# Two graph layers for 16 batch elements: the second layer's attention product as three fp32r terms in place of full f32

## What is computed

```python
feat_proj = jnp.einsum('bnh,oh->bno', feats, fc_w) + fc_b
q = jnp.einsum('bnh,oh->bno', feat_proj, q_w) + q_b
k = jnp.einsum('bnh,oh->bno', feat_proj, k_w) + k_b
logits = q + jnp.swapaxes(k, 2, 1)
masked = logits + (1.0 - adj_mat) * NEG_INF
masked = jnp.where(masked >= 0, masked, LEAKY_SLOPE * masked)
atten = jax.nn.softmax(masked, axis=-1)
out = jnp.einsum('bnm,bmh->bnh', atten, feat_proj)
return out + feats
```

## Time and profile before

| | |
|---|---|
| median of 3 runs | 969.0 us (968.88 to 969.69) |
| profiled execution, its own time | 967.7 us |
| its span, first to last instruction | 965.4 us |
| mean granted clock of PE | 0.988 |
| instructions | 22082 |
| busy: PE / ACT / DVE / POOL | 929.8 / 796.7 / 768.6 / 300.4 us |

### The profile page before, as it was taken

One profiled execution on the slowest core, in us unless ns is written; L12 is line 12 of the kernel. 1 busy time (PEld: TensorE's weight loads), 2 busy tenths in 40 slices (PEclk: granted clock), 3 DMA queues, 4 the chain that ended last, 5 costly groups with the idle time before them and its releaser, 6 DMA issues. The chain is left out here.

```text
span 965.4 us, 22082 instructions
## 1 busy us (share of the span) xinstructions
PE 929.8 (96%) x7432; PEld 776.6 (80%) x7432; DVE 768.6 (80%) x2012; ACT 796.7 (83%) x1900; POOL 300.4 (31%) x408
## 2 busy tenths in 40 slices
PE   5889999999999999999999999999999999999966
PEld 4668788788878878888887888888788888887854
DVE  4687979788797988879788887978879797887832
ACT  3768989889897998989888897988889798887923
POOL 0012334323243431424342142433223343322441
PEclk9999999999999999999999999999999999999988
DMA  6677767476675747666574766657467765746100
GB/s 188 140 134 130 132 106 114 128 117 150 110 132 101 117 124 117 140 120 124 111 116 120 121 127 127 118 122 117 126 112 131 130 102 134 116 110 110 44 23 22
DMA packets 74718, 112.59 MB, mean 117 GB/s; under 512 B 7024, under 2 KB 33648, under 8 KB 74608
## 3 DMA queue, kind: packets, MB, share of 16 engines
q1 hardware_dynamic: 74608, 111.18, 59.7%
HBM read 52.44 MB, written 8.39 MB: 63 GB/s over the span
## 5 line engine op out<-in xcount | busy, mean ns | idle before, releaser
L975 DVE CUSTOM_DVE_ANT_0 sm_bank<-sm_bank,masks 128x512 f32<-128x512 f32 x512 | 352.4, 698 | 116.9 <-PE sm_bank L529 113.2
L731 ACT ACTIVATE e<-sm_bank,row_min 128x512 f32<-128x512 f32 x512 | 356.2, 698 | 33.0 <-DVE row_min L975 33.0
L539 PE MATMUL et_bank<-ident,e 128*128 128x128 f32 x2048 | 308.5, 273 | 3.2 <-DVE e_t L983 1.9
L539 PEld LDWEIGHTS et_bank<-ident,e 128*128 128x128 f32 x2048 | 252.1, 140 | 42.2 <-issue 6.8
L529 PE MATMUL sm_bank<-k_stack,q_stack 96*128 96x512 f32 x512 | 247.7, 484 | 5.6 <-DMA k_stack<-kt_lo 3.2
L723 ACT COPY e_t<-et_bank 128x512 f32<-128x512 f32 x272 | 161.2, 593 | 17.6 <-PE et_bank L539 15.9
L983 DVE COPY e_t<-et_bank 128x512 f32<-128x512 f32 x240 | 164.4, 685 | 11.4 <-PE et_bank L539 9.8
L529 PEld LDWEIGHTS sm_bank<-k_stack,q_stack 96*128 96x128 f32 x512 | 97.0, 190 | 36.2 <-issue 26.5
L475 PE MATMUL o_bank<-e_t,v 128*32 128x256 f32 x2048 | 123.8, 382 | 0.0
L508 PE MATMUL shared<-feat,z 128*128 128x256 f32 x512 | 121.8, 381 | 0.8 <-ACT z L669 0.8
L731 ACT ACTIVATION_READ_ACCUMULATOR e<-sm_bank,row_min 128x1 f32 x512 | 107.4, 210 | 0.0
(11 more groups left out here) (112 smaller groups left out, 1576.6 us busy)
## 6 DMA issues: line engine op xcount, KB each, us to landing
adj_in<-in_adj SPq DMA_DIRECT2D x32, 1024.0 KB, 5.5
q_stack<-qt_hi SPq DMA_DIRECT2D x62, 256.0 KB, 8.0
k_stack<-kt_hi SPq DMA_DIRECT2D x62, 256.0 KB, 7.8
x_in<-in_x SPq DMA_DIRECT2D x16, 512.0 KB, 6.4
h<-in_x SPq DMA_DIRECT2D x16, 512.0 KB, 3.8
out_y<-h SPq DMA_DIRECT2D x32, 256.0 KB, 6.7
q_stack<-qt_lo SPq DMA_DIRECT2D x31, 256.0 KB, 7.1
k_stack<-kt_lo SPq DMA_DIRECT2D x31, 256.0 KB, 11.1
```

The lines of the kernel that those rows point to most:

```text
L539: last = nc.tensor.transpose(et_bank[n % TURNED][:, c * P:(c + 1) * P], e[:, n % ROOM, c * P:(c + 1) * P], ident[:, :])
L731: nc.scalar.activation(e[:, k, :], sm_bank[n % SCORED][:, :], ACT.Exp, scale=-1.0, bias=row_min[:, k:k + 1], accum_out=row_sum[:, g, qt, i ...
L975: nc.vector.tensor_tensor_reduce(bank[:, :], bank[:, :], mask[b % 2][:, qt * N:(qt + 1) * N], 1.0, -LOWEST, ALU.add, ALU.min, row_min[:, k ...
```

## The change

The `at` steps become sums of three fp32r terms, as the projections are: 12 products of one pass for each block of 128 rows in place of 4 full f32 products. For that, `feat` becomes `feat_hi` and `feat_lo`, and the transposed z goes into new tiles `zt_hi` and `zt_lo` instead of back into z. ACT's copies write the hi parts; DVE gets two new kinds of step, `feat_lo0`, `feat_lo1` (two subtractions of 128x256 each) and `et_lo0` to `et_lo3` (one of 128x512 each). The readers that free a shared bank change with it. All five tables, DVE_COPIED (15 tiles before, 14 after), BANK, and the order of steps within a tile are laid out anew. The core of the diff:

```diff
-DVE_COPIED = (0, 3, 5, 6, 13, 14, 15, 18, 22, 24, 25, 26, 27, 28, 29)
+DVE_COPIED = (1, 3, 4, 6, 7, 13, 14, 15, 17, 21, 22, 24, 25, 31)
-FIRST_QK, AFTER_QK = 15, 17
+FIRST_QK, AFTER_QK = 14, 18
 PE_AT = {
-    "at3": 64, "et1": 65, "k1": 2, "rb1": 36, "pv3": 36, "at0": 69, "v1": 6, "at1": 73, "v0": 9, "xt1": -22, "op1": 44,
-    "xt0": -18, "op0": 46, "k0": -17, "q0": -16, "pv0": 17, "ht1": 50, "ht0": 50, "rb0": 21, "fc0": 53, "fc1": 54,
-    "kb": 56, "pv1": 24, "q1": -5, "pv2": 29, "et2": 62, "et3": 62, "at2": 63, "et0": 63}
+    "et1": 65, "v0": 5, "v1": 8, "xt1": -21, "pv1": 24, "q1": -5, "pv2": 29, "et3": 61, "et0": 63, "at3": 64,
+    "rb1": 35, "at1": 74, "op1": 45, "op0": 45, "ht1": 51, "fc0": 53, "fc1": 54, "kb": 55, "rb0": 25, "et2": 60,
+    "k1": 1, "pv3": 36, "at0": 73, "xt0": -21, "q0": -18, "k0": -16, "pv0": 18, "ht0": 50, "at2": 62}
 ACT_AT = {
+    "k_hi1": 2, "v1": 8, "x_hi1": -22, "q_hi0": -17, "h_hi0": 50, "logit0": 56, "lexp2": 58, "et3": 60, "et0": 62,
+    "et1": 64, "rs1": 34, "v0": 7, "hn0": 49, "hn1": 49, "h_hi1": 50, "feat0": 52, "feat1": 53, "logit1": 56,
+    "rs0": 24, "q_hi1": -6, "et2": 59, "o_hi0": 34, "o_hi1": 35, "x_hi0": -22, "k_hi0": -16, "logit2": 55,
+    "logit3": 55, "l_negmax": 56, "lexp3": 58, "lexp0": 59, "lexp1": 61}
 DVE_AT = {
-    "l_recip": 64, "rc1": 33, "fin1": 66, "k_lo1": 4, "o_n1": 38, "fin0": 73, "x_lo1": -20, "h_add1": 45, "stats1": 45,
-    "x_lo0": -18, "h_add0": 46, "stats0": 46, "moments": 46, "k_lo0": -17, "q_lo0": -16, "rc0": 18, "h_lo1": 50,
-    "h_lo0": 50, "q_dot0": 54, "q_dot1": 56, "l_max0": 56, "l_max1": 56, "o_n0": 26, "q_lo1": -4, "mask1": -1,
-    "mask0": -1}
+    "fin1": 64, "rc1": 33, "et_lo1": 66, "k_lo1": 4, "o_n1": 37, "x_lo1": -21, "x_lo0": -20, "q_lo0": -15,
+    "q_dot0": 54, "feat_lo0": 54, "l_max0": 56, "q_lo1": -4, "et_lo2": 61, "fin0": 74, "h_add1": 45, "stats0": 46,
+    "q_dot1": 54, "mask0": -2, "stats1": 45, "h_add0": 45, "moments": 46, "k_lo0": -15, "rc0": 18, "h_lo0": 51,
+    "h_lo1": 51, "l_max1": 55, "feat_lo1": 57, "o_n0": 26, "et_lo3": 61, "mask1": -2, "l_recip": 63, "et_lo0": 63}
 SP_AT = {
-    "adj": 1, "x": -30, "adj_again": 39, "stack1": 18, "store1": 85, "store0": 91, "x_again": 27, "stack0": -4}
+    "store1": 68, "adj_again": 37, "stack1": 6, "store0": 78, "stack0": -12, "x_again": 25, "x": -38, "adj": -5}
...
 READ_BY = {
-    "fc0": ("dve", "q_dot0"), "fc1": ("dve", "q_dot1"), ... **{f"et{c}": ("act", f"et{c}") for c in range(NT)}}
+    "fc0": ("dve", "feat_lo0"), "fc1": ("dve", "feat_lo1"), ... **{f"et{c}": ("dve", f"et_lo{c}") for c in range(NT)}}
...
             def attend(c, b):
-                pe.wait_ge(act_done.sem, max(act_done.of(f"et{c}", b), act_done.all("feat", b)))
+                pe.wait_ge(dve_done.sem, max(dve_done.of(f"et_lo{c}", b), dve_done.all("feat_lo", b)))
...
-                for kt in range(NT):
-                    last = nc.tensor.matmul(bank[:, k * D:(k + 1) * D], z[:, c, kt * P:(kt + 1) * P], feat[:, kt, :],
-                                            start=(kt == 0), stop=(kt == NT - 1))
-                last.then_inc(pe_done.sem, 1)
+                three_terms(bank[:, k * D:(k + 1) * D],
+                            lambda kt: ((zt_hi[:, c, kt * P:(kt + 1) * P], zt_lo[:, c, kt * P:(kt + 1) * P]),
+                                        (feat_hi[:, kt, :], feat_lo[:, kt, :])), NT).then_inc(pe_done.sem, 1)
...
             def turned_z(c, b):
-                copy(z[:, c, 0:N], f"et{c}", bank_of[f"et{c}"][:, :], b)
+                act.wait_ge(pe_done.sem, pe_done.of(f"at{c}", b - 1))
+                copy(zt_hi[:, c, :], f"et{c}", bank_of[f"et{c}"][:, :], b)
...
             def query_logits(half, b):
-                dve.wait_ge(pe_done.sem, pe_done.all("at", b - 1))
+                dve.wait_ge(pe_done.sem, pe_done.all("et", b - 1))
...
+            def features_low(half, b):
+                dve.wait_ge(act_done.sem, act_done.of(f"feat{half}", b))
+                for k in range(2):
+                    c = 2 * half + k
+                    last = nc.vector.tensor_tensor(feat_lo[:, c, :], bank_of[f"fc{half}"][:, k * D:(k + 1) * D], f(feat_hi[:, c, :]),
+                                                   ALU.subtract)
+                last.then_inc(done, 1)
+
+            def turned_low(c, b):
+                dve.wait_ge(act_done.sem, act_done.of(f"et{c}", b))
+                nc.vector.tensor_tensor(zt_lo[:, c, :], bank_of[f"et{c}"][:, :], f(zt_hi[:, c, :]), ALU.subtract).then_inc(done, 1)
```

More of the change, by code:

```diff
@@ L129 @@
 BANK = {
-    "at2": 1, "k1": 0, "v0": 1, "op0": 0, "op1": 1, "v1": 1, "xt0": 1, "xt1": 0, "q0": 0, "ht0": 0, "ht1": 1, "k0": 1,
-    "fc0": 0, "fc1": 1, "kb": 0, "q1": 0, "et0": 0, "et1": 0, "at0": 0, "et2": 1, "et3": 0, "rb0": 1, "rb1": 1}
+    "et1": 0, "v0": 0, "v1": 1, "xt1": 0, "q1": 0, "et3": 0, "et0": 0, "rb1": 0, "op1": 0, "op0": 1, "ht1": 1,
+    "fc0": 0, "fc1": 1, "kb": 0, "rb0": 0, "et2": 1, "k1": 1, "at0": 1, "xt0": 1, "q0": 0, "k0": 1, "ht0": 0,
+    "at2": 1}
 BANK["at1"], BANK["at3"] = BANK["at0"], BANK["at2"]
@@ L136 @@
     "op0": ("dve", "h_add0"), "op1": ("dve", "h_add1"), "ht0": ("dve", "h_lo0"), "ht1": ("dve", "h_lo1"),
[1 row of a table removed]
-    "at2": ("dve", "fin1"), "rb0": ("act", "rs0"), "rb1": ("act", "rs1"), **{f"et{c}": ("act", f"et{c}") for c in range(NT)}}
[1 row of a table added]
+    "at2": ("dve", "fin1"), "rb0": ("act", "rs0"), "rb1": ("act", "rs1"), **{f"et{c}": ("dve", f"et_lo{c}") for c in range(NT)}}
 def build(nc, x, adj, wq, bq, wk, bk, wv, bv, wo, bo, gamma, beta, fc_w, fc_b, q_w, q_b, k_w, k_b, out):
@@ L203, in build @@
         rstd = sb("rstd", [P, NT])
-        feat = sb("feat", [P, NT, D])
+        feat_hi = sb("feat_hi", [P, NT, D], F32R)
+        feat_lo = sb("feat_lo", [P, NT, D], F32R)
+        zt_hi = sb("zt_hi", [P, NT, N], F32R)
+        zt_lo = sb("zt_lo", [P, NT, N], F32R)
         z = sb("z", [P, NT, N + 2])
@@ L333, in iteration @@
                         sp.wait_ge(setup_pe, 7)
[L334 to L339, removed]
+                    if (b := due(SP_AT, "store1", s, t)) is not None:
+                        store(1, b)
                     if (b := due(SP_AT, "adj_again", s, t)) is not None:
@@ L352, in iteration @@
                         sp.dma_start(h[b % 2][:, :, :], rows(x, b)).then_inc(h_loaded.sem, 16)
-                    if (b := due(SP_AT, "stack0", s, t)) is not None:
-                        stack(0, b)
+                    if (b := due(SP_AT, "x", s, t)) is not None and b > 0:
+                        sp.wait_ge(pe_done.sem, pe_done.all("xt", b - 1))
+                        sp.dma_start(x_in[:, :, :], rows(x, b)).then_inc(x_loaded.sem, 16)
+                    if (b := due(SP_AT, "adj", s, t)) is not None and b > 0:
+                        sp.wait_ge(dve_done.sem, max(dve_done.all("mask", b - 1), dve_done.all("l_max", b - 2)))
+                        sp.dma_start(adj_in[:, :, :], rows(adj, b)).then_inc(adj_loaded.sem, 16)
             program(iteration)
@@ L591, in iteration @@
                         turn(u, t + off)
+                    if (b := due(PE_AT, "k1", s, t)) is not None:
+                        project_qk("k", WK, 1, b)
                     if (b := due(PE_AT, "pv3", s, t)) is not None:
@@ L607, in iteration @@
                         turn_h(0, b)
-                    if (b := due(PE_AT, "pv1", s, t)) is not None:
-                        times_v(1, b)
-                    if (b := due(PE_AT, "et3", s, t)) is not None:
-                        turn_z(3, b)
-                    if (b := due(PE_AT, "et0", s, t)) is not None:
-                        turn_z(0, b)
+                    if (b := due(PE_AT, "at2", s, t)) is not None:
+                        attend(2, b)
             program(iteration)
@@ L1021, in iteration @@
                         qk_lo("q", 0, 0, qt_lo, qt_hi, b)
+                    if (b := due(DVE_AT, "q_dot0", s, t)) is not None:
+                        query_logits(0, b)
+                    if (b := due(DVE_AT, "feat_lo0", s, t)) is not None:
+                        features_low(0, b)
+                    if (b := due(DVE_AT, "l_max0", s, t)) is not None:
+                        layer1_maxima(0, b)
+                    if (b := due(DVE_AT, "q_lo1", s, t)) is not None:
+                        qk_lo("q", 1, 0, qt_lo, qt_hi, b)
+                    if (b := due(DVE_AT, "et_lo2", s, t)) is not None:
+                        turned_low(2, b)
+                    if on(t, 0):
+                        masked_minima(s, t)
+                    if (b := due(DVE_AT, "fin0", s, t)) is not None:
+                        finish(0, b)
+                    if (b := due(DVE_AT, "h_add1", s, t)) is not None:
+                        add_residual(1, b)
+                    if (b := due(DVE_AT, "stats0", s, t)) is not None:
+                        statistics(0, b)
+                    if (b := due(DVE_AT, "q_dot1", s, t)) is not None:
+                        query_logits(1, b)
```

(2 more changed lines are left out.)

274 lines of the change are left out of this document (133 added, 141 removed), and 14 rows, old and new, of tables (ACT_AT, POOL_AT, READ_BY).

## The result

The changed kernel takes 963.0 us (median of 4, 961.2 to 965.1) against 969.35 us: ratio 0.9931 [0.9915, 0.9947]. In a later series beside the experiments it took 961.0 us against 970.5, 0.9900 [0.9878, 0.9922]. It is faster, by 6.4 us in one series and 9.5 in the other where I forecast 17.4, and 963.0 lies above my range. So the spans differ by only 2.4 us where the medians differ by 6.4.

The account below looks back on a forecast made before the run. PE, busy without a gap in the periods, was taken as the bound. Terms of -16.8 (56 steps), -1.2 and -0.7 (tail) and +1.3 (stalls) gave -17.4 us: 950.3, or 951.5 us as median; range 947 to 961.

Parts of the forecast that it names:

- PE bounds the periods: Main forecast for the steady periods: PE stays the bound, 948 to 955 us, chance 0.62.
- The attend step: On PE, each step of attention times features goes from 1.73 to 1.43 us, saving 0.30; four save 1.20 per period.
- The low parts: On DVE, per batch four zt_lo subtractions at 0.60 us and four feat_lo at 0.38, less one 0.60 copy: 3.3 us.
- no steady row has PE waiting for zt_lo or feat_lo: Sign in the waits after: no new row with PE behind DVE's zt_lo or feat_lo.
- My period of 56.4 us: Length of one batch element's work before, from twelve periods between 162.7 and 839.4 us; forecast to become 55.2 us.
- I allow 0.1 us per period, 1.3 us in all.: Allowance in the periods for ACT or DVE lag reaching PE, first at a score product or a transpose.
- a rival (0.4 to 0.9 us per period, 956 to 964): DVE and ACT at 90 to 91% stall PE, ACT's excess in tiles 21 to 31 partly coming through; chance 0.22.
- the crowd of tiles 21 to 31: Stretch where new DVE work falls: DVE about 21.0 us, PE 21.1, ACT 22.5, over PE's time by 1.4 us.
- I price both at nothing: SP's queue laid out anew and POOL's changed steps before the last mask were both forecast to cost 0 us.
- My cover: Why SP and POOL cost nothing: POOL works 18.4 of 56.4 us, loads land a tile or more early, adj in 5.5.
- Forecast -1.9 us: The tail: batch 14's four steps save 1.2 us, batch 15's change comes to -0.7 us together.
- the wait for zt_lo: In batch 15, et_lo2 stands between ACT's copy and the first attend step: +0.7 us.

Follow-up runs that it names:

- The kernel with the old product: The changed kernel's new order and tables with the full f32 product of before and without the six low-part steps: 979.9 us, 1.0115 of the kernel before.
- the control: The changed kernel unchanged, run once more on the chip of another experiment: 961.0 us against 970.5 for the kernel before.
- three orders around h: Changed kernel (961.0 us); its evictions of h behind the exponential (960.7 us); that with adj ahead of x and fc0 behind its tile's transposes (958.1 us).

## Why the prediction was wrong

**Right.** PE bounds the periods, but for the stall. The attend step costs 1.44 us for 1.73, and by subtraction the period without its stall is 1.21 us shorter where I had 1.20. The low parts cost what the nearest rows said: one of 128x512 0.68 us, a pair of 128x256 0.74 where I had 0.76. DVE stands at 49.9 us of a period, ACT at 48.9 (forecast 50.5 and 49.7), and no steady row has PE waiting for zt_lo or feat_lo. The 0.119 us per product came out again, not the 109 ns that the Trainium skill (TensorE: Matmul & The Clock Gate, "Back-to-back issue gap") gives for an isolated product at the full clock. That page warns of the stationary loads; no run here takes them away, so what makes the difference is not shown.

My period of 56.4 us was misread: 676.7 us hold 11.93 periods of 56.70, not twelve, so what I divided by twelve is 0.5% low (DVE had 47.5 us, ACT 49.4), and the forecast for the new period should have been 55.5, not 55.2.

**Wrong, the main step:** "I allow 0.1 us per period, 1.3 us in all." It measured 0.55, in 13 periods 7.2 us. I had named the victim, a score product that waits for the exponential, and even its price as a rival (0.4 to 0.9 us per period, 956 to 964). But I looked for the cause in the crowd of tiles 21 to 31, by busy time. It lies ahead of that stretch, in ACT's order: two evictions of h, themselves waiting for a transpose, stand ahead of an exponential. The kernel with the old product has the same stall with DVE at 81%, and moving the evictions takes it away. A walk through ACT's new order from hn to tile 21 against PE's should have led there: 2.06 us for h, one exponential, 0.54 us of waiting for the transposes, 1.26 for the two evictions, and only then the exponential that PE's score product of tile 21 wants. That 963.0 falls into that rival's 956 to 964 is luck in part: some 9 of the ledger's 15 missing us come from places that it does not speak of.

**Wrong: "I price both at nothing"** (SP's queue and POOL). In the periods it holds: no row there has PE or DVE waiting for a load or for POOL. My cover was the landing time of the earlier trace rows, 5.5 us, a median over all periods; in batch 1's row this load took 13.1 us already before, and adj now goes last, takes 16.11 and is wanted 11.0 us behind its issue. Batch 1's row came out 3.9 us longer instead of 0.6 shorter: DVE's wait of 5.2 us reached PE as 3.9, and one stall of 0.55 lies in the row. Putting adj ahead of x took 4.2 us off DVE's wait and 3.0 off the time.

**Wrong: the tail.** Forecast -1.9 us, and -2.5 with the two steps that the ledger counts there; +1.1 came. Of these 3.6 us, 1.0 lies in the four last steps, the first of which ran at 1.2 GHz. The last row of scores has PE waits of 0.8 us for the exponential, 0.3 for a transpose's bank and 0.2 for z, where before had one of 0.7 for h. From its second to its last score product it takes 50.87 us, and 50.87 and 50.88 in two more profiles of this order of PE's steps (the control, and adj ahead of x), so it is not chance; none of it was tried apart, and the rest stays open. I had priced the wait for zt_lo at 0.7 and it took 0.69; that it also leaves PE idle while the clock is low I had not priced.

**Open.** The start (+2.2 and -1.1 us in this pair of executions) varies between executions of the same order by as much. Why three orders around h end at 55.94 to 56.04 is shown as three waits, but whether an order exists that reaches 55.49 was not found. POOL's new order was not tried by itself.

## What to carry to other kernels

When an engine's order is laid out anew, its cost isn't the sum of busy times: walk each engine's new row, at the places where it waits itself (here ACT before the evictions of h), up to the next thing that the bounding engine wants. When you move a transfer in its queue, price it in the fullest stretch, here the head, with everything that now stands ahead of it and with the distance from its issue to its use, and not by a median landing. And read a stall from start to start against an undisturbed neighbour (0.91 to 0.36); the idle time that the view gives was half of it.

## What was not expected of the hardware

Twelve products that take 1.43 us in the periods took 2.70 us at a granted clock of 0.50 behind an idle time of 5.2 us, a short burst of transposes and another 0.69 us of waiting; before, with no second wait, the clock was up within the step. That the second wait held it down is what the two traces suggest; no run tried it alone. A load of 1 MB issued behind six stack loads landed in 13.1 to 13.2 us, and with another 1 MB between them and it in 16.1, where the median of the kernel was 5.5.
